# The last expert in halves, the second attention begun on the first half, and its output weight in f16 parts: one change to a fused layer pair on one core

## The reference

```python
x = x + _L0_attn_ref(_layernorm(x, axis=-1), ...)               # gated linear attention
x = x + _L0_xattn_ref(_layernorm(x, axis=-1), ctx_1024, ...)    # cross attention
x = x + _L0_ffn_ref(_layernorm(x, axis=-1), ...)                # small attention, then 8 experts, top 2
x = x + _L1_attn_ref(_layernorm(x, axis=-1), wq, wk, wv, wo, rel_bias)
x = x + _L1_xattn_ref(_layernorm(x, axis=-1), ctx_1024, ...)
x = x + _L1_ffn_ref(_layernorm(x, axis=-1), ...)
```

```python
h_mid = jax.nn.gelu(jnp.einsum('th,ehf->etf', x, moe_w1))       # 8 experts, 128 -> 256
expert_out = jnp.einsum('etf,efh->eth', h_mid, moe_w2)          # 256 -> 128
moe_out = jnp.einsum('eth,et->th', expert_out, weights)
```

```python
q, k, v = shape(h @ wq), shape(h @ wk), shape(h @ wv)
scores = jnp.einsum('bhqd,bhkd->bhqk', q, k) + position_bias
attn = jax.nn.softmax(scores, axis=-1)
out = jnp.einsum('bhqk,bhkd->bhqd', attn, v)
return out.transpose(0, 2, 1, 3).reshape(b, s, 1024) @ wo
```

## Time and profile before

| what | value |
|---|---|
| median of 3 runs | 499.3 us (499.12 to 499.97) |
| the profiled execution, its own time | 501.62 us |
| span of the profiled execution | 499.5 us |
| busy: PE, DVE, ACT, POOL | 444.7, 372.1, 286.4, 157.3 us |
| last expert's hidden layer begins | 194.09 us |
| first scores of the second attention | 218.40 us |
| first output tile, last output tile begin | 421.99 us, 450.34 us |

### The profile page before, as it was taken

One profiled execution on the slowest core, in us unless ns is written; L12 is line 12 of the kernel. 1 busy time (PEld: TensorE's weight loads), 2 busy tenths in 40 slices (PEclk: granted clock), 3 DMA queues, 4 the chain that ended last, 5 costly groups with the idle time before them and its releaser, 6 DMA issues.

```text
span 499.5 us, 12607 instructions
## 1 busy us (share of the span) xinstructions
PE 444.7 (89%) x4396; PEld 307.7 (62%) x4396; DVE 372.1 (74%) x1005; ACT 286.4 (57%) x618; POOL 157.3 (31%) x398
## 2 busy tenths in 40 slices
PE   3879868888776999489999999999999999999897
PEld 1225455656772777336676666767666767888656
DVE  3746858998677799858787868787878877547666
ACT  3752324664437599258777777777777767313460
POOL 5050011370024365502553455344533433111200
PEclk9959988999997899879999999999999999999999
DMA  7289822600000112100000000000000000000001
GB/s 214 59 98 99 101 25 89 218 24 1 0 2 13 32 53 75 32 1 0 18 18 2 3 16 16 0 0 0 0 0 0 1 1 2 3 2 0 1 0 43
DMA packets 15616, 15.74 MB, mean 32 GB/s; under 512 B 1348, under 2 KB 12859, under 8 KB 15579
## 3 DMA queue, kind: packets, MB, share of 16 engines
q1 hardware_dynamic: 15579, 15.24, 14.8%
HBM read 10.52 MB, written 4.72 MB: 31 GB/s over the span
## 4 chain that ended last, share of the span: by engine, by line
PE 70%; DVE 21%; ACT 5%; issue 3%; DMA 1%; DVEq 0%; SPq 0%; ACTq 0%
PE bank L882 16%; PE bank L1327 11%; PE bank L1278 9%; PE bank L1214 5%; PE bank L1178 3%; PE bank L1165 3%; PE bank L1320 3%; PE bank L1228 3%; PE bank L1210 2%; DVE PX L1627 2%; DVE mx L1625 2%; PE bank L991 2%; PE bank L1439 1%; PE bank L887 1%; DVE stats L1466 1%
## 5 line engine op out<-in xcount | busy, mean ns | idle before, releaser
L796 ACT ACTIVATE SN<-SN,nmx 128x512 f32<-128x512 f32 x128 | 92.8, 725 | 9.4 <-DVE nmx L1827 8.4
L882 PE MATMUL bank<-cs,SN 128*128 128x128 f32 x512 | 67.5, 274 | 1.6
L882 PEld LDWEIGHTS bank<-cs,SN 128*128 128x128 f32 x512 | 57.0, 141 | 17.2 <-issue 11.6
L536 POOL TENSOR_TENSOR CTX<-YT 128x128 f32 (+1 forms) x64 | 29.2, 457 | 117.1 <-DVE YT L1825 117.1
L1278 PE MATMUL bank<-TK,TQ 64*128 64x512 f16 x384 | 52.6, 379 | 0.0
L1812 DVE CUSTOM_DVE_ANT_0 SN<-bank,strip 128x512 f32<-128x512 f32 x64 | 43.2, 675 | 1.3 <-PE bank L1278 1.3
L1827 DVE CUSTOM_DVE_ANT_0 SN<-bank,strip 128x512 f32<-128x512 f32 x64 | 43.5, 680 | 0.0
L1820 DVE COPY PTO<-bank 128x512 f32<-128x512 f32 x32 | 22.1, 691 | 19.7 <-PE bank L1327 19.7
L1820 DVE COPY Z<-bank 128x512 f32<-128x512 f32 x32 | 22.1, 691 | 19.4 <-PE bank L1327 19.4
L1327 PE MATMUL bank<-PTO,TV 128*64 128x128 f32 x512 | 33.4, 273 | 0.0
L1327 PE MATMUL bank<-Z,TV 128*64 128x128 f32 x512 | 33.3, 273 | 0.0
(11 more groups left out here) (306 smaller groups left out, 942.0 us busy)
## 6 DMA issues: line engine op xcount, KB each, us to landing
bias_rows<-biasr SPq DMA_DIRECT2D x1, 4096.0 KB, 44.4
band<-bias_rows SPq DMA_DIRECT2D x1, 3072.0 KB, 12.9
wqkv<-in_twqkv SPq DMA_DIRECT2D x8, 192.0 KB, 2.7
w1s<-in_w SPq DMA_DIRECT2D x8, 128.0 KB, 2.2
w2s<-in_w SPq DMA_DIRECT2D x8, 128.0 KB, 2.1
...
```

The source lines that it names most:

```text
L536: gp.tensor_tensor(dst, raw[:, 0:P], raw[:, P:2 * P], ALU.mult).then_inc(sm["ctt_ready"], 1)
L796: sc.activation(p, p, ACT.Exp, bias=nmx[:, r % RING, h:h + 1], scale=-1.0, accum_out=psm[:, r % RING, h:h + 1]).then_inc(sm["exp_ready"], 1)
L882: return nc.tensor.transpose(out_, in_, ident[0:n, 0:n])
```

## The change

1. **Last experts by halves.** PE does the last expert's hidden layer and both last experts' output one half of the tokens at a time (`last_hidden`, `half_out`), the half outputs in banks 5, 2, 6 and 7, with the transposes of WQ and 14 f32 matmuls of ones (`keep_busy(0, 14)`) in between. ACT does the gelus of the last expert in the order first half, second half (`LAST_ORDER`), and its expert loop is one turn shorter, the rest written out.
2. **Attention begun on the first half.** DVE brings the first half of X to its end, norms it and lets PE project q and k of it before the second half's sums. The second half is normed inside steps 0 to 2 of the attention, and its projections stand in steps 2 and 3. `PROJECTIONS` is now q0, k0, v0, q1, k1, v1, and jobs stand in steps 5, 6, 7 and 1, 2, 3 of every eight.
3. **Output weight and CTX in f16 parts.** POOL makes three instructions for every CTX tile (f32 product into CTW, high part, low part), and in steps 6 to 13 of the last body two more for each pair's block of WO (into WOP). PE's output tile is 24 f16 matmuls instead of 8 f32 ones.
4. Smaller: POOL splits the projection weights ahead of the strips; two semaphores are shared.

```diff
-PROJECTIONS = [("q", 0), ("k", 0), ("q", 1), ("k", 1), ("v", 0), ("v", 1)]
+PROJECTIONS = [("q", 0), ("k", 0), ("v", 0), ("q", 1), ("k", 1), ("v", 1)]
-FIRST_BANKS = (6, 7, 4, 5, 6, 7)
+FIRST_BANKS = (5, 3, 6, 7, 6, 7)
+LAST_ORDER = (0, 2, 1, 3)
...
@@ POOL
-                    pool.wait_ge(sm["raw_ready"], n - 4)
-                    gp.tensor_tensor(dst, raw[:, 0:P], raw[:, P:2 * P], ALU.mult).then_inc(sm["ctt_ready"], 1)
+                    pool.wait_ge(sm["ctt_ready"], RING + n - 5)
+                    pool.wait_ge(sm["raw_ready"], n - 4)
+                    gp.tensor_tensor(CTW[:, :], raw[:, 0:P], raw[:, P:2 * P], ALU.mult).then_inc(sm["ctw_ready"], 1)
+                    pool.wait_ge(sm["ctw_ready"], 2 * n - 9)
+                    gp.tensor_tensor(dst[:, 0, :], CTW[:, :], ones[:, 0:1].to_broadcast([P, P]), ALU.mult).then_inc(sm["ctw_ready"], 1)
+                    pool.wait_ge(sm["ctw_ready"], 2 * n - 8)
+                    gp.tensor_tensor(dst[:, 1, :], CTW[:, :], dst[:, 0, :], ALU.subtract).then_inc(sm["ctt_ready"], 1)
+                pair = s - LAG
+                if last and pair < PAIRS:
...
+                    gp.tensor_tensor(WOP[:, 0, c], WO[:, pair, :], ones[:, 0:1].to_broadcast([P, P]), ALU.mult).then_inc(sm["ow_ready"], 1)
+                    pool.wait_ge(sm["ow_ready"], 2 + 2 * pair)
+                    gp.tensor_tensor(WOP[:, 1, c], WO[:, pair, :], WOP[:, 0, c], ALU.subtract).then_inc(sm["ow_ready"], 1)
...
@@ PE
-            hidden(NE - 1, 1)
-            for u in range(2):
-                expert_out(NE - 2 + u, u)
+            last_hidden(0)
+            pe.wait_ge(sm["hid_lo"], (NE - 2) * 4 + 4 + 4)
+            pe.wait_ge(sm["acc_ready"], 2 * NE - 3)
+            half_out(NE - 2, 0, 0, 5)
+            last_hidden(1)
+            pe.wait_ge(sm["hid_lo"], (NE - 1) * 4 + 2 + 4)
+            half_out(NE - 1, 1, 0, 2)
...
+            keep_busy(0, 14)
+            pe.wait_ge(sm["acc_ready"], 2 * NE)
+            half_out(NE - 2, 0, 1, 6)
...
+            pe.wait_ge(sm["gel_ready"], NE * 4 + 4)
+            projected_norm(0)
+            pe.wait_ge(sm["hid_lo"], NE * 4 + 4)
+            half_out(NE - 1, 1, 1, 7)
+            pe.wait_ge(sm["ln_yt"], 9)
...
                 for p in range(PAIRS):
-                    ins = mm(bank[out_bank(tile)][:, 0:P], CTX[:, p, P * tile:P * tile + P], WO[:, p, :], start=(p == 0), stop=(p == PAIRS - 1))
+                    for k, (c_part, w_part) in enumerate(PRODUCTS):
+                        ins = mm(bank[out_bank(tile)][:, 0:P], CTX[:, p, c_part, P * tile:P * tile + P], WOP[:, w_part, P * p:P * p + P],
+                                 start=(p == 0 and k == 0), stop=(p == PAIRS - 1 and k == 2))
...
+                if s == 1:
+                    projected_norm(1)
+                if s == 2:
+                    pe.wait_ge(sm["ln_yt"], 10)
+                    pe.wait_ge(sm["acc_ready"], 2 * NE + 2)
+                    project(3, 0, FIRST_BANKS[3])
+                    pe.wait_ge(sm["pj_hi"], 3)
+                    project(4, 0, FIRST_BANKS[4])
...
@@ DVE
+            done = 2 * (NE - 3) + 2
+            gated_half(NE - 3, 0, 5, done + 3, done - 1)
+            hidden_low(NE - 1, 1, LAST_ORDER, (0, 1))
+            gated_half(NE - 2, 0, 5, done + 5, done + 1)
+            gated_half(NE - 1, 0, 2, done + 6, done + 2)
...
+            norm_stats(5, 0, X)
+            gated_half(NE - 3, 1, 6, done + 4, done)
+            norm_rows(5, 0, X, Y)
+            hidden_low(NE - 1, 1, LAST_ORDER, (2, 3))
...
+            projected_low(0)
+            gated_half(NE - 2, 1, 6, done + 7, done + 4)
+            gated_half(NE - 1, 1, 7, done + 8, done + 5)
...
 def t5_job(s, last):
-    j, ahead = s % ROWS - JOBS_FROM, s // ROWS + 1
-    if 0 <= j < JOBS and not (last and ahead > 1):
-        return j, ahead % 2, ahead
+    at, ahead = s % ROWS, (s + TG) // ROWS
+    if s >= TG and at % TG != 0 and not (last and ahead > 1):
+        return (at + TG) % ROWS - 1 - (at < TG), ahead % 2, ahead
     return None
```

245 lines of the change are left out of this document (151 added, 94 removed).

## The result

The changed kernel takes 494.5 us (median of 4 runs, 493.63 to 496.06) against 499.6 us for the kernel before on the same chip: a ratio of 0.987, with a 95% interval from 0.9847 to 0.9901. By the medians it is faster by 5.1 us, less than the 7.8 us forecast. (The two medians alone give 0.990, at the upper end of the interval; the recorded ratio of 0.987 would be 6.3 us.) The predicted 491.5 us is 3.0 us too low; the recorded range holds the result, the forecast's own range (up to 493.2) doesn't.

A forecast was written before the change was run, and what follows sets the result against it. PE bounds the attention and output tiles, DVE the seam between experts and attention. Span 499.5 less 4.9 (seam) and 2.9 (output) is 491.7, median 491.5 us; own range 489.8 to 493.2, recorded 489.8 to 495.5.

The forecast's parts named there:

- a fall of the clock: Rival at the new seam: PE half idle, clock falls, first projections slow; 2.6 us more, 494.1 us; chance 0.17.
- a lesser overlap: Rival at the seam: late ACT casts lengthen DVE's chain by 2 to 3 us, gain halves, 494 us; chance 0.13.
- The seam to the first scores: Experts to attention: DVE's chain lets first scores start at 210.7 against 218.40, 7.7 us sooner.
- First scores to step 5: Start of attention: 14.3 us instead of 13.5, so step 5 starts at 225.0, 6.9 us sooner than before.
- four more jobs behind it: Attention behind step 5: four more pair 1 projection jobs at 0.5 us each give back 2.0 us.
- The steps keep their length otherwise, as the jobs' waits are of the same kind.: Attention steps: 3.5 us with a projection and 3.0 without stay unchanged, no further cost.
- A tile "1.36 instead of 1.98": Output: 24 f16 matmuls, priced as twice twelve at 0.68 us, save 0.62 a tile; seven tiles give 4.3 us.
- Waits before tile 0 and tile 5: Output: PE waits for POOL's context and weight work, losing 1.0 us at tile 0 and 0.4 at tile 5.
- No single gap above 1.9 us: Argument against the clock's fall at the seam: no longer PE gap is left, and 2.34 us had not lowered it.
- POOL: Attention body: two new instructions add 1.08 us a step, 2.5 in all, nobody waits; rival about 512 us, chance 0.04.
- The base of the sum: Whole kernel: span 499.5 us less both gains is 491.7; runs' median taken as 0.2 below the span, 491.5.
- what the prediction made of this rule: Seam: by the exclusion rule both low parts wait behind weight splits, first scores about 1 us later; prediction kept 0.17 each.

The follow-up runs named there:

- pool_late: Changed kernel with POOL's weight splits and strips held until DVE has written the last expert's first two low parts; 494.35 us, 0.9878 of before.
- best_3: Changed kernel, RH two steps later, output weight split earlier, POOL kept off both low-part pairs, first value projection before first scores; 493.25 us, 0.9852 of before.
- f32_out: Changed kernel without its third part: context and output weight f32 as before, seam and job order as changed; 496.67 us, 0.992 of before.
- rh_later: Changed kernel with DVE computing RH two steps later in the last body, step 12 instead of 10; 493.03 us, 0.9853 of before.
- only_f16_out: Kernel before with only the third part, context and output weight in f16 parts; 498.76 us, 0.996 of before.
- no_fill: Changed kernel without the filler line keep_busy(0, 14); 497.14 us, 0.993 of before.

## Why the prediction was wrong by 3 us, by its own steps

Between the last hidden layer and the last transposes it forecast 7.8 us less, and 5.7 came. That the recorded range, up to 495.5, holds 494.5 is luck: it was made that wide for a fall of the clock and for a lesser overlap, and neither came. The term that did come was in no rival. The forecast's own range had no working either: the bounds of its two terms add up to 489.0 to 495.3 us, and it gave 489.8 to 493.2.

- **The seam to the first scores** (forecast -7.7, measured -7.34): right, and 0.36 us of it mis-sized. DVE's chain ends, from the anchor on, 0.36 us later than worked out; on the way its members are up to 0.6 us late. Two prices beside POOL were too low. The two low parts cost 0.73 us more (2.01 against 1.28), not twice 0.17; most of it was slack, but the output that needs them starts 0.24 us later than in pool_late. And the four normed rows, for which I had 1.05 us, take 1.59 beside POOL's strips; those of the second half, with POOL idle, take 1.11. In best_3, where POOL stays out of the low parts and of most of the rows, stretch a is 16.46 us, just under the forecast's 16.6. The low parts of the second half ran with POOL idle.
- **First scores to step 5** (forecast +0.8, measured +0.59), **four more jobs behind it** (+2.0; f32_out's stretch c, without the 1.76 of RH, is 1.93 longer than before): right.
- **"The steps keep their length otherwise, as the jobs' waits are of the same kind."** This is the step that failed. It looked at what the jobs wait for, and not at who waits for the jobs. One line did, outside the diff, against a count of all jobs, in DVE's queue at step 10. Price: 1.77 us (rh_later), of the 2.1 us between forecast and measurement by the stretches.
- **A tile "1.36 instead of 1.98"**: mis-sized. It is 1.44, 0.54 saved for 0.62. The 1.36 was twice the start-to-start of twelve matmuls in the projections; measured, a tile of 24 is 1.43 or 1.44 before scores and 1.35 before transposes, where the f32 one is 1.98 and 1.89, so I compared one neighbour with the other: twelve f16 matmuls in front of transposes with an f32 tile in front of scores. Stretch d shows -3.39 for the forecast's -3.9, 0.5 us of the error.
- **Waits before tile 0 and tile 5**: forecast 1.0 and 0.4, measured 0.70 and 0.29, within bounds; tile 7's gain is lost as forecast (only_f16_out shows the same -3.40 in stretch d alone).
- **The clock**: the rival did not come in the changed kernel, 1.00 from 192 to 232 us. It was nearer than my argument said: without the filler, or with one projection moved (best_3), it fell. "No single gap above 1.9 us" was true of the changed kernel, but it left little room: best_3's gap is 1.98 us.
- **POOL**: no effect in the body, as forecast (three instructions at 0.46, 0.40 and 0.43 us; POOL is busy 122.55 of 182 us from 232 to 414).
- **The base of the sum.** 499.5 was taken as the profiled execution's time, "0.2 above the median". That span belongs to an execution of 501.62 us, 2.3 us above the median of 499.3: outside the span lie some 1.8 to 2.1 us in every run here (495.03 against 493.2, 493.4 against 491.6). The sum from the median, 499.3 - 7.8, is 491.5 too, so the number didn't suffer; that is luck, as spans and runs were matched by accident.

Taken together: 7.8 - 0.36 (seam) + 0.2 (to step 5) - 1.77 + 0.3 (tile 0) - 0.5 (tiles) = 5.7 us. The medians say 5.1 on the first chip and 5.5 on the second; the 0.2 to 0.6 below 5.7 are within an interval of 1.4 us to each side. So the 3.0 us by which 491.5 was too low are 2.1 of these steps, 0.3 by which the median of before came out higher this time (499.6 for 499.3), and 0.6 within the noise.

On the two rules of the Trainium skill. In the changed kernel a low part, POOL's split, the second low part and a strip start one after another (196.12, 196.26, 196.72 and 197.53 us). The first takes its usual 0.69 us; the others take 1.32, 1.40 and 0.96 where they have 0.92, 0.69 and 0.51 alone. The Trainium skill (SBUF — State Buffer, "Who interferes with whom") has the two engines exclude each other, the later waiting for the earlier; the trace agrees, as every one but the first is longer. It did not cost what the prediction made of this rule: one low part waited and not both, and the first scores were not 1 us later for it.

For the clock, the trace of before shows eight transposes in 2.14 us behind the gap of 4.33, where eight transposes of the attention take 1.04. In no_fill the 24 matmuls right behind the gap of 3.22 us take 1.77 instead of 1.51, and only then come four transposes in 1.09 instead of 0.63 and a half output in 2.37; in best_3, too, the first group behind the gap of 1.98 us is not slowed. The Trainium skill (TensorE: Matmul & The Clock Gate, "HAM oscillation") says that gaps between bursts re-throttle the engine and the next burst starts slow. The trace of before agrees with both halves; no_fill and best_3 agree that the clock falls, but there the next burst had begun before it fell.
